# SyncE sends the inverse row sums back before the last strip of row maxima, in the attention of a four-layer image kernel

## The reference, cut to what matters

```python
xn = group_norm(x, gn_gamma, gn_beta)
qkv = jnp.einsum('bchw,oc->bohw', xn, w_qkv).reshape(B, 3, nh, d, H * W)
q, k, v = (qkv[:, 0], qkv[:, 1], qkv[:, 2])
scores = jnp.einsum('bhci,bhcj->bhij', q, k) * d ** (-0.5)
attn = jax.nn.softmax(scores, axis=-1)
out = jnp.einsum('bhij,bhcj->bhci', attn, v).reshape(B, C, H, W)
proj = jnp.einsum('bchw,oc->bohw', out, w_proj) + b_proj[None, :, None, None]
return xn + proj
```

## Time and profile before

| | |
|---|---|
| median of 3 runs | 5413.81 us (5411.34 to 5429.07) |
| the profiled execution's own time | 5390.97 us |
| its span | 5389.2 us |
| busy: PE, DVE, ACT, POOL | 4833.2, 3850.9, 3166.0, 3103.1 us |
| mean granted TensorE clock | 0.952 of full speed |

### The profile page before, as it was taken

How to read it: one execution, slowest core, us unless ns; L and a number is a source line. 1 busy time by engine, 2 the same in 40 slices (tenths; PEclk the granted TensorE clock), 3 DMA queues, 4 the chain that set the end, 5 groups by cost and what they waited for, 6 DMA issues and landing times. The chain is left out here.

```text
span 5389.2 us, 73627 instructions
## 1 busy us (share of the span) xinstructions
PE 4833.2 (90%) x21100; PEld 2217.8 (41%) x21100; DVE 3850.9 (71%) x6144; ACT 3166.0 (59%) x5196; POOL 3103.1 (58%) x2581
## 2 busy tenths in 40 slices
PE   7999999997999999999878779879978996998788
PEld 3333333322433333332356657635534553554344
DVE  4788888863588888885333334468978886898898
ACT  2788898883388888988111111145545554554555
POOL 0566666663066666667167667656545654664775
PEclk9999999998999999999878889989989998999999
DMA  2011111111011111111234345489978997998998
GB/s 74 5 9 9 9 9 9 9 9 66 2 7 9 9 9 9 7 7 11 67 106 128 112 141 163 133 312 383 371 277 340 385 382 300 381 383 342 402 410 355
DMA packets 364678, 828.94 MB, mean 154 GB/s; under 512 B 106438, under 2 KB 174020, under 8 KB 364158
## 3 DMA queue, kind: packets, MB, share of 16 engines
q0 software_dynamic: 193536, 679.59, 33.4%
q1 hardware_dynamic: 170878, 146.09, 12.6%
HBM read 724.77 MB, written 100.74 MB: 153 GB/s over the span
## 5 line engine op out<-in xcount | busy, mean ns | idle before, releaser
L1906 DVE TENSOR_REDUCE arena<-ps 128x2 f32<-128x1024 f32 x1024 | 1251.7, 1222 | 412.1 <-PE ps L895 411.6
L795 POOL DMA_INDIRECT arena<-corners,arena x1152 | 1099.2, 954 | 686.5 <-issue 297.3
L744 POOL TENSOR_TENSOR arena<-arena 128x1024 f32<-128x1024 f32 x480 | 1189.2, 2477 | 350.6 <-ACT arena L1380 330.7
L1380 ACT ACTIVATE arena<-ps 128x1024 f32<-128x1024 f32 x1024 | 998.5, 1024 | 249.1 <-PE ps L916 188.8
L2134 DVE SCALAR_TENSOR_TENSOR ps<-arena,ps 128x256 f32<-128x256 f32 x2304 | 955.7, 482 | 234.2 <-DVEq L2128 211.7
L1242 PE MATMUL ps<-arena 128*128 128x512 f32 x2304 | 1051.3, 600 | 0.2
L916 PE MATMUL ps<-arena 64*128 64x512 f32 x4096 | 1018.4, 612 | 28.2 <-ACT ps L1353 28.1
L1353 ACT ACTIVATE ps<-arena 128x1024 f32<-128x1024 f16 x1020 | 1003.9, 1023 | 0.0
L930 PE MATMUL ps<-arena 128*64 128x512 f32 x4096 | 994.2, 606 | 0.0
L1568 ACT ACTIVATE ps<-arena 128x256 f32<-128x256 f32 x1152 | 499.5, 469 | 457.4 <-DMA arena<-corners,arena 203.9
L1924 DVE TENSOR_TENSOR arena<-arena 128x1024 f32<-128x1024 f32 x480 | 624.3, 1301 | 126.3 <-ACT arena L1380 126.3
(11 more groups left out here) (165 smaller groups left out, 3663.3 us busy)
## 6 DMA issues: line engine op xcount, KB each, us to landing
corners<-arena SPq DMA_DIRECT2D x256, 256.0 KB
arena<-corners,arena POOLq DMA_INDIRECT x1728, 6.2
img<-in_x SPq DMA_DIRECT2D x8, 1024.0 KB, 9.4
arena<-row_buf SPq DMA_DIRECT2D x32, 256.0 KB, 4.5
corners<-arena SPq DMA_DIRECT2D x128, 64.0 KB, 2.2
arena<-inv_buf SPq DMA_DIRECT2D x60, 128.0 KB, 10.1
arena<-in_wd SPq DMA_DIRECT2D x2, 2304.0 KB, 8.4
between<-img SPq DMA_DIRECT2D x4, 1024.0 KB, 6.3
```

What stands on the lines that cost most here:

```text
L744: pool.tensor_tensor(SUMS[u % 2][:, 0], SUMS[u % 2][:, 0], PAIR[g % 2][:, :, 0], ALU.add).then_inc(sum_a, 2)
L795: pool.indirect_dma_start(G3[4 * k + t].rearrange("p a c -> p (a c)"), None, table256[b], bass.IndirectOffsetOnAxis(ap=IS3[:, k, t:t + 1], ...
L1380: af(P[n % 4].rearrange("p h q -> p (h q)"), ps[:, 2 * (n % 2):2 * (n % 2) + 2, :].rearrange("p h q -> p (h q)"), ACT.Exp, scale=float(D) ...
L1906: v.tensor_reduce(mxp[i % 2][:, :, j], ps[:, 4:6, :], AX.X, ALU.max).then_inc(mx_done, 1)
```

## The change

In each pass of SyncE's loop `spread_inverses(u - 2)` moves from behind `send_row(u, 3)` to directly behind `send_inverses(u - 2)`. Nothing is added or removed. `spread_inverses` begins with a wait for the landing of the inverses (L449), so this wait now stands in front of the last strip. The passes u = 2 to 15 of each image are reordered, 28 in all; in passes 0, 1 and 16 the order of the instructions stays the same.

```diff
                         send_row(u, 2)
                     if u >= 2:
                         send_inverses(u - 2)
+                        spread_inverses(u - 2)
                     if u < BLOCKS:
                         send_row(u, 3)
-                    if u >= 2:
-                        spread_inverses(u - 2)
-                    if u < BLOCKS:
                         spread_rows(u)
```

## The result

The changed kernel takes 5330.57 us (median of 4 runs, 5324.57 to 5341.29), beside 5418.9 us (now four runs, 5411.34 to 5429.07) for the kernel before: a ratio of 0.9838, 95% interval 0.9814 to 0.9862. That is 88 us, where 50 were forecast, and outside the predicted range. The traced execution took 5341.29 us, where 5341 was forecast, against 5390.97 in the trace of before. So the step looked right in the trace and too small in the runs; the experiments had to tell why. Lines behind the edited loop moved up by two: L1378 of after is L1380 of before, L742 is L744, L708 is L710.

The account below looks back on a forecast made before the run. Bound: the loop of seed, scores and exponential between ScalarE and TensorE, plus one stall a block behind late RC. Removing 48.1 + 1.9 = 50.0 us gave 5413.8 - 50.0 = 5364 us, range 5352 to 5392.

Parts of the forecast that it names:

- The stall and its cause: Once a block ScalarE's pair 15 waits for GpSimd, whose `normalized` waits for late RC; 1.8 us in each of 28 blocks.
- `RC` in time at 412.5: Moved broadcasts land at about 412.5, at the latest 420.4; GpSimd wants RC at 421.3 in the block shown.
- GpSimd's load hidden: At pairs 13 and 14, `normalized` plus addition take 3.1 us within 4.20: no cost; uncovered, 39 us.
- the added wait covered: SyncE's wait for the inverses, now before the last strip, falls in 5 us of its idling: no cost.
- the fold's pattern: GpSimd's same load elsewhere in the trace, 0.73 + 2.36 us; L710 was to follow it, idling about 1 us before.
- `MWIDE` next, with 2.0 us of margin: Next block's transfer lands at 427.4, first seed needs it at 429.36; cost nothing. Rival of it coming late: chance 0.10.
- No later pair gives any of it back: In ScalarE's timeline no pair is shorter than 4.20 us, so the whole stall counts as time of the span.
- sum 50.0: Total stall removed over both attentions: 48.1 + 1.9 = 50.0 us, 1.8 us for each of 28 blocks.
- the beat: Usual 4.20 us between ScalarE's pairs of exponentials, set by the loop seed, scores, exponential between ScalarE and TensorE.
- the 22.8 us: Median of the runs of before above their profiled execution; stage unknown, carried over unchanged into the forecast.
- theory C: From the experiments: before's extra time is longer stalls, followed by TensorE's lower clock; no chance given.
- theory E: Rival throughout the experiments: before's extra time lies elsewhere, outside the loop over pairs; no chance given.

Follow-up runs that it names:

- Hold: Kernel before, SyncE still standing until the last strip is cast, but the two RC broadcasts issued ahead of that strip; 5331.45 us, ratio 0.9907.
- late15: Kernel before with SyncE's order kept, GpSimd doing both `normalized` at pair 15 instead of pairs 13 and 14; 5343.9 us, ratio 0.9924.
- the dosed one: Changed kernel with a transfer of 32 pieces of 4 bytes added ahead of the last strip; 5328.14 us, ratio 0.9910.
- the doses: Kernel before with 32, 64 or 128 pieces of 4 bytes added ahead of the last strip; 5405.57, 5441.81 and 5421.17 us.

## Why the prediction was right or wrong

*The stall and its cause: right.* The RC broadcasts were late because a strip stood in front of them on the queue. Hold lets them pass the strip and gets the whole gain; late15 wants `RC` later and gets 40 of the 48 us.

*`RC` in time at 412.5, GpSimd's load hidden, the added wait covered: right.* 2.9 us of landing, the fold's pattern in L708, the last strip at its old distance from the inverses.

*`MWIDE` next, with 2.0 us of margin: right for this kernel.* No first seed waits for it in after; only 128 added pieces bring such a wait, once in an image.

*"No later pair gives any of it back", sum 50.0: too small by 9.3 us in the loop.* Beyond the beat the 28 stalls do come to 50.0 us. But I looked for pairs shorter than the beat and not for longer ones: six stalls were followed by pairs at the lower clock, which went with the stalls.

*The step that failed: the 22.8 us by which the runs of before lay above their traced execution, "I carry this over as it stands".* The runs of after don't have them: their median, 5330.57, lies 10.7 us below their own traced execution. The 22.8 and the 10.7 make up the 33 us by which the forecast of 5364 was too high, and the low end of the range, 5352, stood on the same offset. The fourth run of before added the other 5 us of the 38 that lie between 50 and 88.

Where the 22.8 us lay stays open. The loop of after is 2158.3 to 2158.9 us in four traces, the dosed one among them, while that of before goes from 2204.2 to 2218.2 in six: this variation the changed kernel has lost. The rest of the span, 3161 to 3181 us over all traces of the study, varies as much in either order, and mostly in the stages behind the second attention: 2824.2 us at a granted clock of 0.918 in the first trace of after, 2811.2 at 0.925 in the one on the third chip. An execution of 5419 us would need a loop of some 2236 to 2256 us (theory C), which the doses produce (2224 to 2271) with after at 5328 to 5339 beside them, or, with a loop as in the six traces, a rest of 3199 to 3213 us (theory E). No undosed trace shows either: none of the five later comparisons caught a before above 5397. Against before on two other chips the forecast of 50 us is met, with 48 and 51 us.

## What to carry to other kernels

A transfer that is issued right behind many tiny writes on the same queue can land late (10.1 us here instead of 2.9): look at what stands ahead of it, not only at when it is issued, and send first what has a reader waiting. A stall that TensorE shares can have a second price, pairs at the lower clock behind it (six of 28 here); count the longer steps behind a stall too. When timed runs and the traced execution disagree, ask which part of the kernel can vary before carrying the difference into a forecast.

## What the runs showed of the hardware that was not expected

128 pieces of 4 bytes take a median of 7.4 us to land, 256 pieces of 16 bytes 2.3 us. A second such strip in front does not add its own 7 us: with 128 pieces more ahead of it (the changed order), the next transfer, which waits for the last strip, goes out 6.7 to 8.6 us behind that strip in 26 blocks, where it takes 7.1 to 8.9 us without them. In two blocks it is 14.06 and 14.28 us.
